# A graph network's max pass: four TensorE signals per round become one, given by a drain

## The reference

```
msgs = z[dst] @ Wd + z[src] @ Ws + edge_weight[:, None] * ww + bm
agg  = segment_max(msgs, dst)
hidden = relu(z @ W1a + agg @ W1b + b1)
x = layernorm(x + hidden @ W2 + b2)
```

## Time and profile before

| what | us |
|---|---|
| median of three runs | 3869.01 |
| the runs | 3853.34, 3870.36, 3869.01 |
| the profiled execution, first to last instruction (span) | 3851.9 |
| gathers of the max pass, first start to last start | 1961.4 to 3185.4 |

### The profile page before, as it was taken

The page is one execution under the profiler, slowest core; times in us unless marked ns, Lnnn a source line. Parts: engine busy times, 40 slices in busy tenths (PEclk is TensorE's granted clock), DMA queues, the critical chain, the costliest instruction groups (busy, mean ns, idle before and its releaser), DMA issues.

```text
span 3851.9 us, 54329 instructions
## 1 busy us (share of the span) xinstructions
PE 3125.2 (81%) x21070; PEld 2150.6 (56%) x21070; DVE 1459.7 (38%) x3223; ACT 958.7 (25%) x2512; POOL 2340.9 (61%) x2327
## 2 busy tenths in 40 slices
PE   3788788878889888888857787878878787999898
PEld 2444444455557677777735555555656564555454
DVE  6555555223222111111224444544444443333333
ACT  2555455122222011010122222322222232000000
POOL 3666662666662665666446666666666662777775
PEclk7899999899999999999955665665665667999899
DMA  5444444655555666666433343433444337666564
GB/s 150 162 160 166 167 149 156 200 175 185 190 181 172 193 193 188 198 193 201 144 112 103 108 116 101 119 102 112 112 127 127 111 113 253 211 226 218 195 225 144
DMA packets 278767, 621.83 MB, mean 161 GB/s; under 512 B 60077, under 2 KB 188649, under 8 KB 270953
## 3 DMA queue, kind: packets, MB, share of 16 engines
q1 hardware_dynamic: 171944, 372.56, 28.5%
q0 software_dynamic: 104832, 244.47, 22.5%
q10 hardware_dynamic: 1728, 1.25, 0.1%
HBM read 477.62 MB, written 140.45 MB: 160 GB/s over the span
## 4 chain that ended last, share of the span: by engine, by line
PE 56%; another core or an unknown queue 15%; issue 13%; DVE 7%; ACT 6%; DMA 3%; SPq 1%; DVEq 0%; POOL 0%; ACTq 0%; POOLq 0%
PE banks L2056 27%; PE banks L1294 5%; PE banks L2077 4%; PE banks L554 3%; PE banks L2075 3%; PE banks L1283 3%; PE banks L1272 3%; PE banks L1274 1%; PE banks L529 1%; PE banks L2170 1%; PE banks L1154 1%; DMA ring_of_rows<-weight_parts 1%; ACT arena L2363 1%; ACT arena L1213 1%
## 5 line engine op out<-in xcount | busy, mean ns | idle before, releaser
L2056 PE MATMUL banks<-arena 128*128 128x384 bf16 (+1 forms) x9310 | 1557.1, 316 | 129.0 <-issue 114.3
L2056 PEld LDWEIGHTS banks<-arena 128*128 128x128 bf16 x9310 | 914.4, 100 | 618.0 <-issue 235.8
L516 POOL DMA_INDIRECT arena<-tab_l,ring_of_rows x831 | 808.4, 973 | 472.3 <-issue 286.3
L2121 POOL DMA_INDIRECT arena<-h_pieces,span_sources x450 | 435.8, 968 | 319.2 <-issue 108.3
L2121 POOL DMA_INDIRECT ring_of_rows<-message_pieces,span_sources x396 | 430.2, 1086 | 214.1 <-issue 98.0
L2121 POOL DMA_INDIRECT ring_of_rows<-x_pieces,span_sources x306 | 332.9, 1088 | 201.3 <-PE banks L2075 101.1
L1294 PE MATMUL banks<-arena 128*128 128x64 f32 x1662 | 349.8, 380 | 123.4 <-issue 123.0
L2101 DVE TENSOR_TENSOR arena<-iota_bf,span_targets 128x768 bf16<-128x768 bf16 x243 | 134.9, 556 | 822.3 <-remote 318.3
L2121 POOL DMA_INDIRECT ring_of_rows<-l_pieces,span_sources x306 | 300.7, 983 | 233.0 <-issue 71.8
L1294 PEld LDWEIGHTS banks<-arena 128*128 128x128 f32 x1662 | 315.9, 284 | 201.5 <-issue 190.4
L1388 DVE TENSOR_TENSOR_SCAN ring_of_rows<-arena,ring_of_rows,banks 128x512 f32<-128x512 bf16 x207 | 264.2, 1277 | 135.6 <-remote 57.7
(11 more groups left out here) (243 smaller groups left out, 3098.4 us busy)
## 6 DMA issues: line engine op xcount, KB each, us to landing
arena<-edge_counts SPq DMA_DIRECT2D x83, 896.0 KB
arena<-edge_counts SPq DMA_DIRECT2D x83, 672.0 KB
edge_counts<-arena SPq DMA_DIRECT2D x32, 1568.0 KB
typed_counts<-arena SPq DMA_DIRECT2D x27, 1568.0 KB
arena<-scan_mask SPq DMA_DIRECT2D x208, 128.0 KB
arena<-typed_counts SPq DMA_DIRECT2D x27, 896.0 KB
arena<-typed_counts SPq DMA_DIRECT2D x27, 672.0 KB
arena<-tab_l,ring_of_rows POOLq DMA_INDIRECT x831
```

The costliest lines, as they stand in the source:

```text
L516: k.nc.gpsimd.indirect_dma_start(k.RG3[:, i % p.ring, at:at + width], None, table, bass.IndirectOffsetOnAxis(ap=k.SRC[:, i:i + 1], axis=0) ...
L2056: t = T.matmul(k.bank[i % N_SUMS][:, 0:rows.shape[-1]], counts[:, s, :], rows, start=s == 0 and n == 0, stop=s == NT - 1 and n == len(term ...
L2121: G.indirect_dma_start(k.rows[p.layer][s % n], None, k.pieces[p.layer], bass.IndirectOffsetOnAxis(ap=k.SRCG[:, at:at + 1], axis=0)).then_i ...
```

## The change

All of it is in the regular path of the max pass.

- TensorE's signals `l2_turned`, `l2_back`, `l2_product` and `typed_counted` are no longer given by the last matmul of each piece of work. At the end of round c there is one drain (an instruction of TensorE's queue that comes to its end when the engine has finished what was issued before it), and the drain adds to a new semaphore `l2_round`. Only the first two chunks' turning (one drain, on `l2_turned`) and the typed units before the pass (by matmul, as before) keep signals of their own.
- All who waited for one of the four now wait for the end of the round in which that work is done (`chunk_turned`, `chunk_selected`, `units_counted`, `round_done`).
- The order of a round is now: nodes' stage, `turn_messages(c + 2)`, `select(c - 2)` (one round later than before, `SELECT_LAG`), nodes' stage, typed counts, nodes' stages, `turn_back(c)`, drain. Two rounds with a `select` and a drain alone follow at the end.
- `one_hots(c)` and `take(c - 3)` are a round and two rounds later; the nodes' steps are put three chunks later.
- The nodes' stages on TensorE are each followed by a drain of their own, which adds to the stage's semaphore.

```diff
+SELECT_LAG = 2
@@ l2_slots
-            while done < end and (NEWEST[done] if regular else min(done, N_ET - 1)) < (c * CH if c < NCH else N_ET):
+            while done < end and (NEWEST[done] if regular else min(done, N_ET - 1)) < ((c - (SELECT_LAG + 1) * regular) * CH if c < NCH else N_ET):
...
+def round_done(k, c):
+    return k.sem("l2_round"), c + 1
+def chunk_turned(k, c):
+    return (k.sem("l2_turned"), 1) if c < 2 else round_done(k, c - 2)
+def chunk_selected(k, c):
+    return round_done(k, c + SELECT_LAG)
+def units_counted(k, n):
+    return (k.sem("typed_counted"), n) if n <= UNITS else round_done(k, n - UNITS - 1)
@@ max_tensor_l2, a nodes' stage (the other three alike)
-            T.matmul(o, k.w1_2[:, 1, :], k.BEST3[:, gslice(g), :], start=False, stop=True).then_inc(p.sem(stage), 1)
+            T.matmul(o, k.w1_2[:, 1, :], k.BEST3[:, gslice(g), :], start=False, stop=True)
+            T.drain().then_inc(p.sem(stage), 1)
@@ max_tensor_l2, the rounds
     turn_messages(0)
     turn_messages(1)
+    T.drain().then_inc(k.sem("l2_turned"), 1)
...
-        if c:
-            select(c - 1)
+        if c >= SELECT_LAG:
+            select(c - SELECT_LAG)
         nodes(k.slots[c][1])
-        turn_back(c)
-        nodes(k.slots[c][2])
         if typed_unit(c):
             tensor_typed_counts(k, *typed_unit(c))
+        nodes(k.slots[c][2])
         nodes(k.slots[c][3])
-    select(NCH - 1)
+        t = turn_back(c)
+        T.drain().then_inc(round_done(k, c)[0], 1)
+    for c in range(NCH, NCH + SELECT_LAG):
+        t = select(c - SELECT_LAG)
+        T.drain().then_inc(round_done(k, c)[0], 1)
@@ max_vector_l2
     scan(0)
-    one_hots(0)
...
             scan(c + 1)
-            one_hots(c + 1)
+        one_hots(c)
...
-        if c:
-            take(c - 1)
-    take(NCH - 1)
+        if c >= SELECT_LAG + 1:
+            take(c - SELECT_LAG - 1)
+    for c in range(NCH - SELECT_LAG - 1, NCH):
+        take(c)
@@ scan, on VectorE
-        V.wait_ge(k.sem("l2_turned"), c + 1)
+        V.wait_ge(*chunk_turned(k, c))
...
-            V.wait_ge(k.sem("l2_back"), c - 1)
+            V.wait_ge(*round_done(k, c - 2))
@@ max_scalar_l2
-        A.wait_ge(k.sem("l2_back"), c + 1)
+        A.wait_ge(*round_done(k, c))
@@ max_gpsimd_l2
-            G.wait_ge(k.sem("l2_turned"), (i - AHEAD) // CH + 1)
+            G.wait_ge(*chunk_turned(k, (i - AHEAD) // CH))
```

More of the change, by code:

```diff
@@ L372, in __init__ @@
         self.stages = REGULAR if regular else STAGES
-        self.product = k.sem(f"{layer}_product")
+        self.product = None if regular and layer == "l2" else k.sem(f"{layer}_product")
         self.added = k.sem(f"{layer}_added")
@@ L531, in turn @@
             n += 1
-    t.then_inc(sem, 1)
+    if sem:
+        t.then_inc(sem, 1)
 def copy_out(k, g, dst, width, banks, sem):
@@ L1155, in tensor_typed_counts @@
                          k.TKEY[quarter % 2][at, c, :], start=True, stop=True)
-    t.then_inc(k.sem("typed_counted"), 1)
+    if i == 0:
+        t.then_inc(k.sem("typed_counted"), 1)
+    return t
 def vector_typed_one_hots(k, quarter):
@@ L1163, in vector_typed_one_hots @@
     if quarter >= 2:
-        V.wait_ge(k.sem("typed_counted"), 2 * (quarter - 1))
+        V.wait_ge(*units_counted(k, 2 * (quarter - 1)))
     if part == 0:
@@ L1207, in scalar_typed_counts @@
     A = k.nc.scalar
-    A.wait_ge(k.sem("typed_counted"), UNITS * i + u + 1)
+    A.wait_ge(*units_counted(k, UNITS * i + u + 1))
     if u == 0 and i >= 2:
@@ L1232, in node @@
             T.matmul(o, k.w1_2[:, 0, :], k.ROWT3[:, gslice(g), :], start=True, stop=False)
-            T.matmul(o, k.w1_2[:, 1, :], k.BEST3[:, gslice(g), :], start=False, stop=True).then_inc(p.sem(stage), 1)
+            T.matmul(o, k.w1_2[:, 1, :], k.BEST3[:, gslice(g), :], start=False, stop=True)
+            T.drain().then_inc(p.sem(stage), 1)
         elif stage == "second":
             T.wait_ge(*p.at("relu", g))
-            products(k, g, lambda q: blocks(k.HT, g, q), [k.w2_2[:]], H, (max_bank(g),), p.sem(stage))
+            products(k, g, lambda q: blocks(k.HT, g, q), [k.w2_2[:]], H, (max_bank(g),), None)
+            T.drain().then_inc(p.sem(stage), 1)
         elif stage == "xturn":
             T.wait_ge(*p.at("normalise", g))
-            turn(k, g, k.xt, H, (max_bank(g),), p.sem(stage))
+            turn(k, g, k.xt, H, (max_bank(g),), None)
+            T.drain().then_inc(p.sem(stage), 1)
         elif stage in ("parts", "parts2") and max_tiles(g, stage == "parts2"):
@@ L1244, in node @@
             for q, j in enumerate(max_tiles(g, stage == "parts2")):
-                t = T.matmul(k.bank[max_bank(g)][:, q * H2:(q + 1) * H2], k.ROWT3[:, j, :],
-                             k.wdc[:, :, :].rearrange("p k h -> p (k h)"), start=True, stop=True)
-            t.then_inc(p.sem(stage), 1)
+                T.matmul(k.bank[max_bank(g)][:, q * H2:(q + 1) * H2], k.ROWT3[:, j, :],
+                         k.wdc[:, :, :].rearrange("p k h -> p (k h)"), start=True, stop=True)
+            T.drain().then_inc(p.sem(stage), 1)
     def nodes(which):
@@ L1273, in turn_messages @@
         T.wait_ge(k.sem(f"load_mask_{c % MASKS}"), 32 * (c // MASKS + 1))
-        T.matmul(bank[:, 0:len(tiles) * P], k.WW9, k.W9[c % MASKS][:, 0:len(tiles) * P], start=False,
-                 stop=True).then_inc(k.sem("l2_turned"), 1)
+        return T.matmul(bank[:, 0:len(tiles) * P], k.WW9, k.W9[c % MASKS][:, 0:len(tiles) * P], start=False, stop=True)
     def turn_back(c):
@@ L1369, in take @@
     def take(c):
-        V.wait_ge(p.product, c + 1)
+        V.wait_ge(*chunk_selected(k, c))
         if c:
@@ L1546, in max_sync_l2 @@
         load_messages(k, p, a, b)
-    S.wait_ge(p.product, NCH)
+    S.wait_ge(*chunk_selected(k, NCH - 1))
     for a, b in SOURCES[1]:
```

6 lines of the change are left out of this document (3 added, 3 removed).

## The result

The changed kernel took 3941.4 us (median of four, 3934.2 to 3947.0) against 3861.2 us (four, 3841.0 to 3870.4) of the kernel before: **ratio 1.023, 95% interval 1.020 to 1.026**. It is slower by 80 us where 111 us less were forecast. The profiled execution has a span of 3930.0 us, 78.1 more than before. The pass, from the first turning to the last select, went from 1246.6 to 1320.1 us, so 73.5 of these lie in it; 7.3 lie behind it, and it starts 2.8 earlier.

The account below looks back on a forecast made before the run. TensorE bounds the pass: 978.5 work, 98 drains and 50 idle make 1126.5 us against 1246, 119.5 less; 9 us come back for the nodes' steps, so 3869 - 111 = 3758 us, range 3688 to 3985.

Parts of the forecast that it names:

- The four signals go: TensorE's idleness in the max pass: one round's lag covers late signals, idle falls from 267.5 to 50, gaining 217 us.
- if drains signal at once: Condition on the max pass's idle estimate: only idleness not from late signals is left, taken as 50 us.
- Rival 2: Drains in the pass come as late as matmuls' signals did, TensorE's queue behind them: 3976 or 3966 us, chance 0.27.
- prompt part of the drains: Drains at rounds' ends and nodes' stages: 279 at 0.35 us each, 98 us, bounds 56 and 167.
- idle from other causes: TensorE in the pass: gathers not landed, weights' transfer and full-clock stretches faster than POOL, 50 us.
- TensorE's work: TensorE's busy time in the max pass, taken as unchanged at 978.5 us.
- the bounds I named: Granted clock of the pass, 0.61 before: the prediction is wrong in size if it leaves 0.55 to 0.7.
- The drain's own price: On TensorE, lost overlap of 0.20 us plus restart of 0.05 to 0.15, taken as 0.35 each, bounds 0.20 to 0.60.
- The nodes' steps: Three chunks later, 11 stages of group 11 come after the last round: 9 us lost, bounds 0 and 15.
- POOL's permission: Gathers' permission moves to the end of round c-2, about 3 us later, for a chunk four further on: no cost.
- Rival 1: POOL becomes the bound of the pass, with drains near 0.2 us and a higher clock: 3692 us, chance 0.13.
- Rival 3: Drains of 0.8 to 0.9 us on 279 places use up the 217 us gained: 3875 to 3912 us, chance 0.13.

Follow-up runs that it names:

- fourth job: Kernel before (3851.1 us) beside the changed kernel, 1.023, the changed order without drains, 1.003, and only select one round later, 1.002.
- first and fourth job: First: against the kernel before (3887.9 us), new order without drains 1.003, with four signals 1.002, rounds' drains only 1.011; old order with silent drains 1.040.
- second job: Kernel before 3360.5 us; changed kernel with two wide typed products 3416.5, split weights' product 3417.3, second drain 3431.4; four-signal new order with cast first 1.004.
- fifth job: Kernel before, 3365.4 us, and the same with a drain that signals nothing at each round's end, 3365.1 us, ratio 1.001.

## Why the prediction was wrong

**The step that failed is "The four signals go"**, the 217 us taken from TensorE's idleness. It had two halves, and the runs contradict both. That a select two rounds behind covers the late signal is true of the select alone (123.0 to 2.1 us). But ScalarE's cast stands behind the same signal, and the slack that I worked out for it, 3.34 us less 1.6, is less than many of the delays: without drains the typed unit stalls for 209.1 us, and the kernel gains nothing in either order, with one signal or four (1.003, 1.002, 1.002). And "if drains signal at once" was a condition that I let stand; it fails in a third of the rounds (71 of 208). The time behind a held drain is lost by the whole of TensorE's queue: TensorE was idle for 254.4 us of the pass, not 50. One reading of the earlier trace rows was wrong as well. "Nothing ran on TensorE in the meantime" is true of the 6.23 us before the select, but not of the 7.58 from `turn_back`'s end to its copy, in which the typed unit and `turn_messages` of the next round ran first: there was work for a late signal to hide behind in the kernel before, and a drain takes it away.

**Rival 2 is what happened**, at about its price (3976 or 3966 against 3941). That the measured time lies inside the stated range, 3688 to 3985, is owed to that rival and not to the forecast's mechanism. It was to decide from 0.53 us on top of the 0.35 of a round. The round's drain costs 0.90 of gap and 0.24 of overlap, 1.14: 0.79 on top. I gave it 0.27 because rows 5 and 6 had been read as the signals' lateness and not as TensorE's. Their own content spoke for it: several signals of different matmuls came in one burst, after nothing had run for 4 us; whatever held them seems to have held all that TensorE had to report, and a drain asks for just that.

The terms of the pass, as forecast and as measured in the profiled execution:

| | forecast | measured |
|---|---|---|
| prompt part of the drains | 98 | some 126: 268 in the pass, each 0.23 of gap and 0.24 of overlap |
| drains held | 0 | 189: 187.5 + 62.6 us of idleness less 268 gaps of 0.23 |
| idle from other causes | 50 | 4, the rest of 254.4 |
| TensorE's work | 978.5 | 1001, at a clock of 0.57 and not 0.61 |
| pass | 1126.5 | 1320.1 |

The drains' two rows are estimates, with 0.23 and 0.24 us for every one of the 268. The work's row is what is left of 1065.7 busy once 64 us of lost overlap (measured at half clock behind `turn_back`) are taken out, and the kernel without drains is busy for 1003 and 1010 us in its two profiles on chips with late signals. The clock of 0.57 means about 185 us of the pass at the full level where 0.61 meant 274; it stayed in the bounds I named, and its price, in the work's row, is the smallest difference of the four.

**The drain's own price** was mis-sized: 0.47 us behind `turn_back` at half clock where I took 0.35, inside the bounds of 0.20 to 0.60. The overlap was about right (0.24 for 0.20), the restart too short (0.23 for 0.05 to 0.15).

**The nodes' steps** at 9 us were about right: 7.3 us behind the pass in the first profile, 4.6 and 6.8 in two others, and 6.2 without drains in the fourth job. They go with the lag, not with the drains, and are the likely reason why even the kernels without drains are 0.2 to 0.5% slower than before, wherever they ran.

**POOL's permission at nothing** held for the pass on a chip with late signals, where `turn_messages` waits only 5.3 us for gathers. But POOL's waits were to shrink to under 60 us, and they grew from 186 to 233.6. On a quick chip, where POOL sets the pace, they are what the drains cost.

**Rival 1**, POOL the bound, is true of the quick chips, but of the kernel before as well, so it left nothing to gain. Rival 3, a constant 0.8 to 0.9, is refuted by the two kinds of drain. Its sum is also off at the lower end: 3869 + 9 + 6 is 3884, and not 3875. Of what would show it, the copy did follow the drain's end within 0.1 us (206 of 208) and the gap did scatter; its mean of 0.90 is just under the 1 us that I had set as the mark, which was too high, since it left out the overlap.

**The Trainium skill's rule** that I weighed (PSUM — Partial Sum Buffer, "Engine vs sequencer instructions") now has rows here. It has the increment on the matmul itself, as a matter of correctness, where it fires when the matmul completes, and gives a drain as a standalone barrier, which waits for the engine to go fully idle. The quick chips agree with the first: signals within 0.1 us. On the others ScalarE's copy starts over 1 us after the modelled end of its `turn_back` in 102 of 208 rounds of the first profile. The drains agree with the second: a gap of 0.22 to 0.24 us behind most of the prompt ones, and more behind a held one. In time, signals by matmuls are the better ones here on both kinds of chip, by 72 and 21 us.

What stays open: what holds TensorE's completions. They come late on the chips of the first profile and of the first and fourth job, and not on those of the other three. On a chip with late ones, which drains are held is not left to chance but repeats with the program: in the changed kernel's two profiles (the first, and the fourth job's) 94 and 91 of the 268 drains of the pass are held over 0.3 us, 86 of them the same ones, 68 of these within 0.1 us of the same length. In the first, 65 of the 71 held drains at rounds' ends are followed by a prompt one, and of the 12 drains behind a group's `second` 10 are held over 1 us (3.4 us on the mean of the 12), of the 12 behind `first` none. So on such a chip the holds go with the kernel's own work, and do not come at times of their own (Theory P of the second job); by which part of that work is not shown. In the first profile's trace no instruction or transfer of another engine was found that goes with the moment of their release. The kernels that were to tell a number of matmuls from a length of time, and whether ScalarE's cast first helps, met chips without holds only. Nor is it shown what the stages' drains cost beyond their overlap, or why a silent drain in the old order has a longer gap behind it (370.4 us in 208 rounds, 1.78 each) than the round's drain in the new (0.90). That the holds make up the whole 500 us between the two kinds of chip is likely (TensorE's busy share between 500 and 1500 us is 84% in the first profile and 93% in the fifth job's) but was not separated from other differences; the granted clock there is 0.93 and 0.98.

## What to carry to other kernels

Where a matmul's signal comes late, expect a drain in its place to come late too, and everything queued behind it with it (here 189 us). Try such an exchange first with a drain that signals nothing, one line, which gave the answer here (4.0%). And when a stall is given slack, look for the next consumer of the same producer: here it took the stall over in both orders tried. Where two chips differ by 14% in one kernel, compare only within one job: the same edit read 4.0% on one kind and 0.1% on the other.

## What was not expected of the hardware

- Chips differ: 3851 to 3888 us for the kernel before in three measurements, 3360 to 3362 in three others. On the slower kind ScalarE's copy started over 1 us after its `turn_back` in 102 of 208 rounds (the kernel before, first profile); on the quicker in none (fifth job).
- Held and prompt drains alternate for stretches (rounds of 5.24 and 6.55 us in turn), and the same ones are held again in another job's profile of the same kernel (86, of 94 and 91).
- A prompt drain costs 0.22 to 0.24 us of gap at either clock, and at half clock 0.24 of overlap behind a 128x128 turn, 0.04 behind the typed unit's short product.
